# One-hots between the block operands, and weight products per pair of blocks, on VectorE of a four-layer graph network

## The reference

```
layer 0: msg = relu([h[src], h[dst], ea] @ mW1 + mb1) @ mW2 + mb2
         agg = segment_sum(msg, dst) / clip(count, 1)
         out = layernorm(relu([h, agg] @ uW1 + ub1) @ uW2 + ub2 + h) * gamma + beta
layer 1: out = h @ W1 + b1 + segment_sum(h[src], dst) @ W2 + b2
layer 2: out = segment_sum(norm * (h @ W)[src], dst) + bias      norm from edge weights and degrees
layer 3: out = h + relu(0.9 * segment_sum(norm3 * h[src], dst) + 0.1 * h)
```

## Time and profile before

| | |
|---|---|
| median of three runs | 948.86 us (948.36 to 949.64) |
| span of the profiled execution | 946.8 us |
| median less span: what lies around the span | 2.06 us |
| the gathers of the sweep (line 769), first and last start | 40.8 and 613.1 us |
| busy share: PE, DVE, POOL, ACT | 90%, 67%, 55%, 54% |

### The profile page before, as it was taken

The page is one execution under the profiler, slowest core; times in us unless marked ns, Lnnn a source line. Parts: engine busy times, 40 slices in busy tenths (PEclk is TensorE's granted clock), DMA queues, the critical chain, the costliest instruction groups (busy, mean ns, idle before and its releaser), DMA issues.

```text
span 946.8 us, 19062 instructions
## 1 busy us (share of the span) xinstructions
PE 851.2 (90%) x6997; PEld 788.9 (83%) x6997; DVE 636.1 (67%) x1758; ACT 510.7 (54%) x1013; POOL 520.9 (55%) x496
## 2 busy tenths in 40 slices
PE   3257889889898978999989999999999999999997
PEld 2257879879898978989989999987889888888886
DVE  6528979887786877779897989968743311115664
ACT  2224757556575656768777788853353011114873
POOL 5477777777777777777777777745110000023110
PEclk9667999999898989999999999999999999999999
DMA  8752556556565666556565556656247778784500
GB/s 206 199 109 71 159 160 209 165 159 214 174 200 158 173 142 192 165 165 204 168 184 156 176 159 196 176 172 195 70 157 274 295 297 299 297 287 139 165 23 27
DMA packets 109503, 168.91 MB, mean 178 GB/s; under 512 B 14723, under 2 KB 69545, under 8 KB 109406
## 3 DMA queue, kind: packets, MB, share of 16 engines
q1 hardware_dynamic: 92062, 137.01, 44.8%
q0 software_dynamic: 13648, 28.21, 11.5%
q10 hardware_dynamic: 3696, 2.42, 0.9%
HBM read 109.15 MB, written 58.44 MB: 177 GB/s over the span
## 4 chain that ended last, share of the span: by engine, by line
PE 43%; POOL 38%; issue 13%; DMA 4%; ACT 1%; SPq 1%; DVE 1%; ACTq 0%; POOLq 0%; DVEq 0%
POOL room L769 36%; PE ps L1889 14%; PE ps L1874 14%; PE ps L1714 2%; DMA room<-p_rows,idx 2%; PE ps L1715 2%; PE ps L1728 2%; PE ps L1858 2%; PE ps L1745 2%; PE ps L1747 2%; PE ps L1650 1%; DMA w_m<-in_L_gnn_mW 1%; POOL pair L769 1%; DMA p_rows<-g 1%; ACTq L905 0%
## 5 line engine op out<-in xcount | busy, mean ns | idle before, releaser
L769 POOL DMA_INDIRECT room<-p_rows,idx x416 | 438.0, 1053 | 137.5 <-issue 125.0
L1714 PE MATMUL ps<-room,ident 128*128 128x128 f32 x832 | 178.8, 299 | 59.7 <-DMA room<-p_rows,idx 58.9
L1714 PEld LDWEIGHTS ps<-room,ident 128*128 128x128 f32 x832 | 135.5, 205 | 63.5 <-DMA room<-p_rows,idx 45.6
L1715 PE MATMUL ps<-room 128*128 128x128 f32 x832 | 170.6, 289 | 0.0
L1745 PE MATMUL ps<-room 128*128 128x200 bf16 x800 | 161.3, 253 | 0.0
L1747 PE MATMUL ps<-room 128*128 128x100 bf16 x1600 | 160.6, 208 | 0.0
L1294 DVE TENSOR_TENSOR room<-room,Wp 128x800 bf16<-128x800 bf16 x300 | 155.4, 571 | 0.0
L1747 PEld LDWEIGHTS ps<-room 128*128 128x128 bf16 x1600 | 147.9, 98 | 3.9
L1889 PE MATMUL ps<-room,h 128*128 128x256 f32 (+1 forms) x650 | 136.2, 371 | 0.0
L1715 PEld LDWEIGHTS ps<-room 128*128 128x128 f32 x832 | 136.0, 205 | 0.0
L927 ACT ACTIVATE g<-ps 128x512 f32<-128x512 f32 x104 | 62.2, 598 | 136.8 <-PE ps L1715 136.7
(11 more groups left out here) (195 smaller groups left out, 1132.1 us busy)
## 6 DMA issues: line engine op xcount, KB each, us to landing
weight_blocks<-room SPq DMA_DIRECT2D x50, 800.0 KB, 4.6
room<-weight_blocks SPq DMA_DIRECT2D x12, 3200.0 KB
room<-dst_row SPq DMA_DIRECT2D x52, 256.0 KB
room<-count_blocks SPq DMA_DIRECT2D x8, 1600.0 KB
count_blocks<-room SPq DMA_DIRECT2D x50, 200.0 KB
room<-p_rows,idx POOLq DMA_INDIRECT x416
first_c<-count_blocks SPq DMA_DIRECT2D x4, 1600.0 KB, 10.0
edge_windows<-room SPq DMA_DIRECT2D x1, 3072.0 KB
```

The costliest lines, as they stand in the source:

```text
L769: return pool.indirect_dma_start(to, None, table, bass.IndirectOffsetOnAxis(ap=at, axis=0))
L1714: pe.matmul(to, ident[:, :], G[:, n % GS, c, :], start=True, stop=False)
L1715: last = pe.matmul(to, sT[:, n % TS, 128 * c:128 * c + 128], Qr[:, n % QS, :], start=False, stop=True)
```

## The change

`block_operands` is taken apart into `mask_operand`, `lo_operand` and `weighed_operands`, and the one-hots and the copy of Q's window are set between them. DVE's iteration for 3 <= q < 103 is now: `add`, (reading of piece A), mask, one-hot 0, Q copy, `sta`, one-hot 1, products of pairs 0 and 1, one-hot 2, products of pairs 2 and 3, one-hot 3, and then what followed before. The products are made by pair: four instructions of 3 parts x 200 = 600 columns in place of three of 800. The wait for the mask through `link` becomes a semaphore of its own, `s_mask`, waited for ahead of the products.

The other lines of the diff are in the branch that runs only when the flag says that the edges do not fit the plan: there `z_set` is replaced by `s_pad` in places, and ACT waits once more for `s_dst4`. With these inputs that branch is not taken.

```diff
-            def block_operands(u):
+            def mask_operand(u):
                 if u >= SETS:
                     dve.wait_ge(s_wmm, 2 * (u - SETS + 1))
-                k = u % SETS
-                link(dve.tensor_tensor(mov[:, k, 0, :, :, :], ..., blocks_of(Kt, u, KCOLS), ALU.is_equal))
-                dve.tensor_tensor(sta[:, k, :, :, :], ..., blocks_of(LOt, u, 128), ALU.is_equal)
-                for a in range(PARTS):
-                    last = dve.tensor_tensor(mov[:, k, 1 + a, :, :, :], mov[:, k, 0, :, :, :],
-                                             blocks_of(Wp[:, a, :], u, KCOLS), ALU.mult)
-                last.then_inc(s_bop, 1)
+                dve.tensor_tensor(mov[:, u % SETS, 0, :, :, :], ..., blocks_of(Kt, u, KCOLS), ALU.is_equal)\
+                    .then_inc(s_mask, 1)
+
+            def lo_operand(u):
+                dve.tensor_tensor(sta[:, u % SETS, :, :, :], ..., blocks_of(LOt, u, 128), ALU.is_equal)
+
+            def weighed_operands(u, half):
+                k = u % SETS
+                dve.wait_ge(s_mask, u + 1)
+                for i in range(NW // 2 * half, NW // 2 * (half + 1)):
+                    by = Wp[:, :, CB * u + 2 * i:CB * u + 2 * i + 2].rearrange("p r (a t) -> p r a t", a=1)
+                    last = dve.tensor_tensor(mov[:, k, 1:1 + PARTS, i, :, :],
+                                             mov[:, k, 0:1, i, :, :].to_broadcast([128, PARTS, KCOLS, 2]),
+                                             by.to_broadcast([128, PARTS, KCOLS, 2]), ALU.mult)
+                if half:
+                    last.then_inc(s_bop, 1)
...
             for q in range(NQ + 1):
+                u = q + 2 - LAG
+                made = 0 <= u < STEPS
                 if q >= 1:
                     add(q - 1)
-                    if q - 1 + LEAD < NQ:
-                        q_window(q - 1 + LEAD)
                     if SLOT.get(q - 1, " ")[0] == "A":
                         read_A_piece(SLOT[q - 1][1], slot_bank(q - 1))
...
-                if q + 1 < NQ:
+                if q < 3:
                     onehot(q + 1)
...
+                split = 3 <= q < NQ - 1
+                if made:
+                    mask_operand(u)
+                if split:
+                    onehot(q + 1, (0,))
+                if q >= 3 and q - 1 + LEAD < NQ:
+                    q_window(q - 1 + LEAD)
+                if made:
+                    lo_operand(u)
+                if split:
+                    onehot(q + 1, (1,))
+                if made:
+                    weighed_operands(u, 0)
+                if split:
+                    onehot(q + 1, (2,))
+                if made:
+                    weighed_operands(u, 1)
+                if split:
+                    onehot(q + 1, (3,))
...
-                if 0 <= q + 2 - LAG < STEPS:
-                    block_operands(q + 2 - LAG)
                 piece_steps(q)
```

More of the change, by code:

```diff
@@ L358, in gnn_kernel @@
         s_add = sem("quad_added")
+        s_mask = sem("block_masks")
         s_bop = sem("block_operands")
@@ L686, in _ @@
                     .then_inc(s_xc[0], 16)
-                sp.wait_ge(z_set, 1)
+                sp.wait_ge(s_pad, 11)
                 sp.dma_start(x[0:NR, NT - 1, :], x_in[128 * (NT - 1):N, :]).then_inc(s_xc[0], 16)
@@ L1131, in _ @@
                 again_sums(0)
+                act.wait_ge(s_dst4, 128)
                 again_sums(1)
@@ L1270, in q_window, with onehot @@
                 dve.tensor_copy(Qr[0:WIN, n % QS, :], q_bank(n)[0:WIN, :]).then_inc(s_Qr, 1)
-            def onehot(q):
-                if q >= OS:
+            def onehot(q, columns=range(4)):
+                if q >= OS and 0 in columns:
                     dve.wait_ge(s_seg, q - OS + 1)
-                for c in range(4):
+                for c in columns:
                     last = dve.tensor_scalar(oh[:, q % OS, c, :], iota[:, :], dstT[:, q, c:c + 1], None, ALU.is_equal)
-                last.then_inc(s_oh, 1)
+                if 3 in columns:
+                    last.then_inc(s_oh, 1)
             def blocks_of(a, u, n):
@@ L1281, in blocks_of @@
                     .to_broadcast([128, NW, n, 2])
-            def block_operands(u):
+            def mask_operand(u):
                 if u >= SETS:
                     dve.wait_ge(s_wmm, 2 * (u - SETS + 1))
-                k = u % SETS
[L1287 to L1290, removed]
+                dve.tensor_tensor(mov[:, u % SETS, 0, :, :, :],
+                                  iota_k[:, :, :].rearrange("p (a c) t -> p a c t", a=1)
+                                  .to_broadcast([128, NW, KCOLS, 2]), blocks_of(Kt, u, KCOLS), ALU.is_equal)\
+                    .then_inc(s_mask, 1)
+            def lo_operand(u):
+                dve.tensor_tensor(sta[:, u % SETS, :, :, :],
                                   iota_l[:, :, :].rearrange("p (a c) t -> p a c t", a=1)
                                   .to_broadcast([128, NW, 128, 2]), blocks_of(LOt, u, 128), ALU.is_equal)
-                for a in range(PARTS):
-                    last = dve.tensor_tensor(mov[:, k, 1 + a, :, :, :], mov[:, k, 0, :, :, :],
-                                             blocks_of(Wp[:, a, :], u, KCOLS), ALU.mult)
-                last.then_inc(s_bop, 1)
+            def weighed_operands(u, half):
[8 more added lines that the diff above has]
+                    last.then_inc(s_bop, 1)
             def unpack():
@@ L1403, in _ @@
             for q in range(NQ + 1):
+                u = q + 2 - LAG
+                made = 0 <= u < STEPS
                 if q >= 1:
                     add(q - 1)
-                    if q - 1 + LEAD < NQ:
-                        q_window(q - 1 + LEAD)
                     if SLOT.get(q - 1, " ")[0] == "A":
                         read_A_piece(SLOT[q - 1][1], slot_bank(q - 1))
+                if q >= 1 and q - 1 + LEAD < NQ and q < 3:
+                    q_window(q - 1 + LEAD)
                 if q == NQ:
                     break
-                if q + 1 < NQ:
+                if q < 3:
                     onehot(q + 1)
@@ L1587, in _ @@
                 dve.wait_ge(s_out, 16 * NC)
[L1588 to L1591, removed]
+                dve.memset(x[:, NT - 1, :], 0.0).then_inc(s_pad, 1)
+                dve.memset(z_dsti[:, NCH - 1:NCH], PAD_DST).then_inc(s_pad, 1)
+                dve.memset(z_w[:, NCH - 1:NCH], 0.0).then_inc(s_pad, 1)
+                dve.memset(z_ea[:, NCH - 1:NCH, :], 0.0).then_inc(s_pad, 1)
                 dve.wait_ge(s_xc[0], 48)
@@ L1594, in _ @@
                 dve.wait_ge(z_ld, 16 * NLOADS)
-                dve.wait_ge(z_set, 5)
+                dve.wait_ge(z_set, 1)
                 link(dve.tensor_copy(z_dstf, z_dsti))
```

1 line of the change is left out of this document (added).

## The result

The changed kernel takes 1000.41 us in the median (995.88 to 1004.09, 4 runs), the kernel before beside it 949.25 (948.36 to 949.68, 4 runs): ratio 1.0521, 95% interval 1.0486 to 1.0555. The prediction of 944.0 was wrong in sign and outside its range. The profiled execution took 1004.09 us, of which 1002.3 are span.

What follows compares the result with a forecast made beforehand. POOL's gathers were taken to bound the sweep until 489 us, then PE. 77 quads x 0.059 = 4.5 us plus 0.4 at the end gave 946.8 - 4.9 = 941.9 us span; with 2.06 around it 944.0, range 935 to 952.

Steps and rivals of the forecast that it cites:

- What bounds the kernel: In the sweep POOL's pace is gather length plus 0.30 us; from 489 us PE sets the pace.
- price formula: A DVE operation of length L costs POOL 0.74 x (L - 0.18)^2 / 2; explains 34 of 45 us.
- The wait for the mask: Replacing `link` behind DVE's mask is free, covered by about 1 us of work; uncovered, 0.1 us per quad.
- One-hots and copy between: Spreading them among DVE's mask, `sta` and products: zero; phase shifts bounded by 0.1 us per quad either way.
- Products by pair: Four DVE products of 454 ns in place of three of 571: POOL saves 0.059 us per quad.
- One-hots and Q copy later: Queued behind the mask on DVE: zero, 2.7 us to spare; without that cover up to 2 us per quad.
- D: Slower: gathers miss a DVE operation's end when a one-hot follows, +0.23 us per quad, 966 us; chance 0.08.
- C: Faster: loose DVE order breaks patterns lengthening gathers, 0.1 us per quad beyond A, about 936.5 us; chance 0.13.
- A: The forecast itself: POOL saves 0.059 us per quad, 944 us, own range 939 to 948; chance 0.50.
- B: No measurable change, 948.9 us: phases or late gather landings cancel the gain, or `tensor_tensor` stalls no gathers; chance 0.22.

Runs made afterwards that it cites:

- order_back: The changed kernel with the copy and all four one-hots in front of the mask again, still no wait behind the mask: 1073.12 us, ratio 1.1258.
- parts_order_back: Nearly the kernel before less its wait behind the mask: old order, three products of 800 columns; 1079.27 us, ratio 1.13.
- pairs_old_order: The kernel before with four products per pair of blocks, old order and wait behind the mask kept: 961.88 us, ratio 1.012.
- wait_before_mask: parts_order_back with DVE waiting for its last one-hot before the mask: 963.95 us, ratio 1.0137.
- link_kept: The changed kernel with the wait through `link` behind the mask put back: 970.87 us, ratio 1.0187.
- link_kept_parts: The changed kernel with the wait behind the mask put back and three products of 800 columns: 959.93 us, ratio 1.0107.
- never_adjacent: The changed kernel with a one-hot ahead of each of the four pair products: 997.94 us, ratio 1.049.
- met_wait: parts_order_back with a wait that is already met behind the mask: 1081.0 us, ratio 1.135.

## Why the prediction was wrong

**What bounds the kernel** was right. POOL's pace in the sweep is the gathers' length plus 0.30 us, and (1349 - 1053) x 416 = 123 us in order_back stands beside 120 us of time (1073 less 953, the kernel before on the same chip), as 52 beside 51 in the changed kernel. The price formula's 34 us stands beside 32 us in a tally of the kernel before, though not operation by operation: the mask lengthens gathers by 10 us where the formula has 5, `sta` by 6.5 for 10, the products by 14 for 17.

**The wait for the mask, "is free"**: the step that failed. I priced `link` by DVE's 0.03 us gap and by what could cover its absence. What it did was done to POOL: it kept the ends of the operations behind it open to gathers (the last section has how far). Its removal alone makes the kernel 13% slower (parts_order_back), the largest effect in this study, and its return to the changed kernel brings the ratio from 1.052 down to 1.019.

**One-hots and copy between, "zero", bounded by 0.1 us per quad**: the bound held as long as the wait stands (6 to 10 us, which is 0.06 to 0.10 us per quad), but the rule behind it failed for the same reason. Without the wait the order is worth 70 to 76 us the other way. Rows 6 show a gather let in at the end of line 1290, before an operation that follows without a gap. I read this as a rule of ends; it was a rule of ends shortly behind a wait. The one wait of DVE on itself in the iteration stands one operation ahead of that row. The whole change cost 0.51 us per quad, five times the bound that I set for phases.

**Products by pair**: length right (454 forecast, 467 measured), value wrong in sign. 0.059 us per quad was to be saved; with the wait kept the pairs cost 8 to 11 us. The price formula takes the phase between gathers and DVE as even, and the tally of pairs_old_order shows it locked: 53 of 100 starts in 0.06 us.

**One-hots and Q copy later, zero**: right. PE's products with the one-hots (line 1759) wait 2.3 us in all, and for "issue", not for DVE.

**The rivals.** D had the right kind of cause, a missed end, at a wrong place (in the changed kernel the mask's end misses none) and a third of the size. Its own row held more than I took from it: the gather of 313.37 missed the end of line 1351 and got in at the mask's end, where the wait stands. C and A had the wrong sign. B's rule of the Trainium skill ("SBUF — State Buffer", Who interferes with whom), the inference that descriptor generation needs the write side and so is not held up by `tensor_tensor`, fails in every run: the gather at 377.33 ran into six `tensor_tensor` operations and waited 2.5 us. The section's rule that such an operation contends with a GpSimd instruction that reads SBUF is not refuted, since the gather's indices lie in SBUF; no run here separates the two.

The Trainium skill ("VectorE: DVE Perf Modes", The DRAIN you can't avoid) says that between chained operations a semaphore "costs nothing extra". The trace differs a little in DVE's own time: in all kernels here the next operation starts 0.08 us ahead of the end of the one before, and 0.03 behind it where DVE waits for that one, as 252.87 against 252.28 + 0.68 = 252.96 above for the first kind. That is 0.11 us a wait; what the wait gave POOL is over ten times as much in each quad (126/100).

**Not settled.** Why a wait opens the ends behind it is not shown. It isn't that the next operation starts later: in wait_before_mask and before, ends are open although it starts 0.08 us ahead. Nor is it the distance from a gather's start to the end (see the last section). How long the effect lasts is known only roughly, and whether operations or time use it up isn't separated. In link_kept four operations lie between the wait and the products, and 40 of the 87 gathers that start in the first product before the second one starts are held over its end; in link_kept_parts, with the same order and 800 columns, 2 of 36. And the two-way price of the pairs was traced to phases by a tally of starts, not by a run that moves a phase alone.

## What to carry to other kernels

A wait of VectorE on its own result, and perhaps any other stop of it, may be what lets GpSimd's gathers in; before one is removed or replaced by a later one, look at how long gathers last that start in the operations behind it, and try that edit alone. An edit in three parts (wait, order, shape) is best timed in all combinations: here the worth of the order and that of the shape changed sign with the wait. That a gather got in at an end once says nothing of the same end when other operations, or no wait, stand ahead of it.

## What the runs showed of the hardware

**Stops of VectorE for PE seem to count too.** In parts_order_back the addition waits for PE, and the mask is the seventh operation behind that stop:

```profile
253.17 0.29 DVE L1265 TENSOR_TENSOR ST<-ST,ps 128x128 f32<-128x128 f32 x1 [5.21 <-PE ps L1730]
253.37 0.28 DVE L1272 COPY room<-ps 125x128 f32<-125x128 f32 x1
253.57 0.86 DVE L1278 TENSOR_SCALAR g<-iota,dstT 128x128 f32<-128x128 f32 x4
254.35 0.56 DVE L1289 TENSOR_TENSOR room<-iota_k,Kt 128x800 bf16<-128x800 bf16 x1
```

I took from all 18 traces the lengthened gathers that met, at least 0.14 us after their start, the end of the operation in which they started, where the next operation followed without a gap. They sort by how many operations VectorE had run since it last stood still, for whatever reason:

| place of the operation behind the last stop | gathers | held over its end |
|---|---|---|
| first to third | 758 | 0 |
| fourth and fifth | 529 | 16 |
| sixth and later | 1073 | 525 |

This also says what the order did. In the old order without the wait the mask stands seventh or later behind the stop in nearly every step. In the changed kernel it mostly stands first (in 64 steps), since it waits there for PE itself (24.1 us in all), and the products then come sixth and later. In never_adjacent 90 of the 94 such gathers that start in a one-hot in the eighth place or later are held. So it need not be the one-hot behind the mask that opens the mask's end in the changed kernel; the stop ahead of it fits all traces. This is read off afterwards; no run moves a wait for another engine alone.

**Distance.** In the three kernels without the wait (order_back, parts_order_back, met_wait) 278 gathers start in the mask or the block one-hot, and whether one gets in at that operation's end goes by its distance: the 76 that do start 0.09 to 0.12, 0.28 to 0.32 or 0.48 to 0.51 us ahead of the end, three narrow bands 0.19 us apart. Of the 202 held over it, 185 start at other distances. An example of one let in, of order_back, 0.08 us into the mask and so 0.48 ahead of its end:

```profile
240.17 0.56 DVE L1289 TENSOR_TENSOR room<-iota_k,Kt 128x800 bf16<-128x800 bf16 x1
240.25 1.30 POOL L770 DMA_INDIRECT room<-p_rows,idx  x1 [0.31 <-issue]
240.66 0.68 DVE L1295 TENSOR_TENSOR room<-iota_l,LOt 128x1024 bf16<-128x1024 bf16 x1
```

Behind a wait gathers get in at other distances too: 25 in before and 39 in wait_before_mask start more than 0.01 us outside the three bands, 0.15 to 0.65 us ahead of the end, and all get in at it. So it is not by moving the gathers into the bands that the wait lets them in. The bands suggest that a held gather asks again each 0.19 us, but its length does not go in such steps: 192 of the 202 held ones, and those behind a wait, are lengthened by the distance to the end at which they got in, less 0.13 us, within 0.02 us. What makes the bands is open.
